# Last gate tile of batch 1 moved to the scan's beginning, reciprocal moved, every second softplus difference made in SBUF

## The chip, the cores and the metric

One NeuronCore of a Trainium2 chip. The time is device microseconds (us) for one execution of the whole kernel. TensorE is PE in the rows (its weight load PEld), VectorE is DVE, ScalarE ACT, GpSimd POOL, SyncE SP. SP and ACT each issue DMAs into a queue of their own.

## The reference

A decoder layer on x of shape (2, 512, 1024): a Mamba block, cross attention over a context of 1024 tokens, and a feed-forward block, each added to its input and followed by a layernorm. The change lies in the Mamba block alone:

```python
proj = hidden_states @ in_proj_w                # -> x and z, each (2, 512, 2048)
xc = silu(causal_conv4(x))                      # depthwise, along the sequence
ssm_p = einsum('bdl,ed->ble', xc, x_proj_w)     # 64 for dt, 16 for B, 16 for C
dt_r, Bm, Cm = rmsnorm of the three pieces
dt = softplus(dt_r @ dt_proj_w.T + dt_bias)     # (2, 2048, 512)
h = exp(dt * A) * h + dt * B * xc               # the scan, 16 states a channel
y = (einsum(h, C) + D * xc) * silu(z)
out = y @ out_proj_w.T
```

Everything is float32. Where a matrix product must be accurate, each operand is split into a rounded part ("hi") and a remainder ("lo"), and three products are summed (`three_passes`, L106).

## The kernel before

The program is written by hand, engine by engine: each engine has one list of instructions, and semaphores order them. A channel tile is 128 channels by 512 tokens; a batch has 16 (`IT`), both have 32 (`NX`).

**The projection stage** (`mamba_in`, 0 to 302 us). PE computes 32 x tiles and then 4 gate (z) tiles of batch 1 (`main(n)`, n = 32 to 35, 24 matmuls each), alternately into PSUM banks 0 and 1. The other gate tiles are made during the scan. Behind each x tile DVE does the convolution in four steps (`conv`, L491, L495), ACT the silu (L392) and the rounding (L398), and PE the x_proj product (`xproj`). Weights come through three slots: SP loads, ACT rounds (`round_w`, L384), POOL makes the remainder (`rest_w`, L599).

After a batch's last x_proj product, ACT squares the result and takes the root (L405 to L410), and DVE normalises (`normalize`: reciprocal L509, products L514 and L515). This frees the dt products on PE (`dt_product(i)`, L684), each for a pair of channel tiles; i = 8 to 15 are batch 1. For each i ACT makes exp(-|v|) (L424, L426) and its logarithm (L434). DVE makes the rounding difference of the exponential (`remainder`: L522 and L524 with the result in PSUM banks 2 and 3 for i >= 8, L527 and L529 with the result in SBUF for i < 8), then `ramp` (L543) and `total` (L549). POOL multiplies the result by xc (`product(i)`, L611), and SP stores dt and u to DRAM.

**The scan** (`mamba_scan`, 302 to 1093 us). 32 iterations (`it`), one a channel tile, of 8 pairs n. For each pair: ACT makes a = exp(dt * A) in PSUM (L1063); POOL makes dbx = u * B (L895); DVE runs the scan (L1092) and multiplies by C (L1081; for two pairs of eight POOL does, L1107); PE sums over the states (L1197). In between PE makes the keys and values of the attention (units "k", L1150, and "v", L1158). The tile it needs dt and u in a spread layout: `load_dt(it)` and `load_u(it)` are four DMAs of 256 KB each.

Iteration 1 needs dt(1) and u(1), which lie over the buffers of x's rounded part and of the dt weights. SP issues these loads (L853) before the key weights wk (1.5 MB, L910), a context chunk (1 MB, L878), the value weights wv (1.5 MB, L912) and a second chunk (1 MB). `product(n)` of the scan on POOL waits for u(it) at the first pair of an iteration, ACT for dt(it).

Of the kernel before, what the change touches and what calls it, by code (L numbers as in the profile page):

```python
# [27 lines left out]
P = 128  # L28
# [84 lines left out]
Projection = namedtuple("Projection", "sync scalar vector gpsimd tensor r_done dt_done")  # L113
# [89 lines left out]
def mamba_in(nc, res, d, ps_all, scan):  # L203
# [51 lines left out]
    par_ld, dtw_ld = sem("par_ld"), sem("dtw_ld")  # L255
# [15 lines left out]
    IN_PSUM = BG  # L271
    BY_POOL = range(IT, NX - 2)
# [11 lines left out]

    def w_tile(n):
        return n % IT if n < NX else IT + n - NX

    def sync(sp):
        def load_w(n):
            if n >= NW:  # L290
                sp.wait_ge(main_done, n - NW + 1)
            sp.dma_start(w[n % NW][:], d["w_in"][w_tile(n)]).then_inc(w_ld[n % NW], 16)

        def load_x(b):
            for k in range(HT):
                sp.dma_start(x[b][:, k], d["x_t"][k, :, b * L:(b + 1) * L]).then_inc(x_ld[b][k], 16)
# [79 lines left out]
        sp.wait_ge(bc_st, 16 * B)  # L376
        sp.wait_ge(z_st, 16 * NF)

    def scalar(act):
        def round_w(n):  # L380
            if n >= NW:
                act.wait_ge(main_done, n - NW + 1)
            act.wait_ge(w_ld[n % NW], 16 * (n // NW + 1))
            nc.scalar.activation(w_hi[n % NW][:], w[n % NW][:], ACT.Copy).then_inc(w_hi_done, 1)  # L384
# [2875 lines left out]
```

## Time and profile before

| | |
|---|---|
| median of 3 runs | 3032.65 us (3032.1 to 3036.48) |
| the profiled execution | 3035.89 us, its span 3034.6 us |
| granted TensorE clock, mean | 0.974 of full speed |
| busy: PE, DVE, ACT, POOL | 93%, 79%, 52%, 60% of the span |
| projection stage | 0 to 302 us |
| scan | 302 to 1093 us |

The profiled execution took 3.2 us more than the median. Rows give start, duration, engine, line, output and input names (buffer numbers left out), and in brackets how long the engine was idle before and who released it. "PEclk" is the granted clock of TensorE: 1.00 is 2.4 GHz, 0.50 is 1.2 GHz. The shares are averages over stages; which engine sets the pace differs from stage to stage.

### The profile page before, as it was taken

How to read it: one execution, taken by the hardware profiler on the slowest of the kernel's cores; microseconds unless marked ns; L12 is line 12 of the kernel's file. 1: busy time of each engine (PE TensorE's matmuls, PEld its weight loads, DVE VectorE, ACT ScalarE, POOL GpSimd, SP SyncE). 2: the span in 40 equal slices, each digit the busy share in tenths (PEclk: the TensorE clock that was granted, in tenths of full speed). 3: DMA queues.
4: the chain of work that ended last, by engine and by line, in shares of the span. 5: the costliest groups of instructions: out<-in, count | busy, mean ns of one | idle time of the engine just before them, and what ended most of it. 6: DMA issues, size and time to landing. Idle time of an engine off the chain costs nothing. (4 is left out here: it accounts for less than half of the span.)

```text
span 3034.6 us, 35492 instructions
## 1 busy us (share of the span) xinstructions
PE 2824.4 (93%) x11950; PEld 2029.5 (67%) x11950; DVE 2386.7 (79%) x2206; ACT 1571.8 (52%) x2722; POOL 1815.3 (60%) x1068
## 2 busy tenths in 40 slices
PE   8996788888788989999999999999989999999997
PEld 6773344343222357888888888878768888887886
DVE  6677999999999968444777777765988888875677
ACT  4566455555665544214888888873433333334443
POOL 3474999999999943403888888861044444430034
PEclk9997899999989999999999999999989999999999
DMA  5457986665875644331111111225245555567654
GB/s 193 125 181 225 290 199 168 175 165 148 263 208 146 197 177 174 118 118 62 35 36 37 37 37 37 71 69 191 92 157 180 181 180 181 180 218 239 195 178 138
DMA packets 221699, 455.41 MB, mean 150 GB/s; under 512 B 34381, under 2 KB 48461, under 8 KB 219661
## 3 DMA queue, kind: packets, MB, share of 16 engines
q1 hardware_dynamic: 184942, 402.27, 42.7%
q10 hardware_dynamic: 36576, 50.87, 5.1%
q8 instruction: 97, 1.59, 0.2%
q14 instruction: 84, 0.69, 0.1%
HBM read 322.89 MB, written 130.15 MB: 149 GB/s over the span
## 5 line engine op out<-in xcount | busy, mean ns | idle before, releaser
L2105 POOL TENSOR_TENSOR at_p_lo<-at_p,at_p_hi 128x512 fp32r<-128x512 f32 x384 | 514.7, 1348 | 241.9 <-ACT at_p_hi L1998 234.1
L895 POOL TENSOR_TENSOR scan_dbx<-scan_u,scan_b_bc 128x1024 f32<-128x1024 f32 x256 | 596.4, 2364 | 1.6 <-DMA scan_u<-u 1.6
L1063 ACT ACTIVATE mamba_ps<-scan_dt,scan_a_neg 128x512 f32<-128x512 f32 (+1 forms) x512 | 332.0, 680 | 313.0 <-DVE scan_g L1081 289.4
L1092 DVE TENSOR_TENSOR_SCAN mamba_ps<-mamba_ps,scan_dbx 128x1024 f32<-128x1024 f32 x195 | 439.9, 2283 | 7.3 <-ACT mamba_ps L1065 6.0
L2025 DVE TENSOR_REDUCE at_neg_max<-heads_ps 128x1 fp32r<-128x1536 f32 x128 | 225.0, 1758 | 134.2 <-PE heads_ps L2117 132.3
L2990 POOL TENSOR_TENSOR ff_raw<-ff_raw,ff_scale 128x512 f32<-128x512 f32 x112 | 116.3, 1069 | 356.2 <-DMA ff_raw<-in_w 247.7
L108 PE MATMUL heads_ps<-ff_x_hi,ff_w_hi 128*128 128x512 f32 x784 | 309.8, 395 | 17.5 <-DVE ff_u L2750 6.6
L109 PE MATMUL heads_ps<-ff_x_lo,ff_w_hi 128*128 128x512 f32 x784 | 307.9, 393 | 0.0
L110 PE MATMUL heads_ps<-ff_x_hi,ff_w_lo 128*128 128x512 f32 x784 | 307.7, 393 | 0.0
L1994 ACT ACTIVATE at_p<-heads_ps 128x512 f32<-128x512 f32 x384 | 228.2, 594 | 109.9 <-PE heads_ps L2141 95.7
L1998 ACT ACTIVATE at_p_hi<-at_p 128x512 fp32r<-128x512 f32 x384 | 242.7, 632 | 12.2
L1167 PE MATMUL mamba_ps<-scan_x,scan_wz 128*128 128x512 f32 x448 | 216.8, 629 | 23.2 <-ACT scan_zb L984 16.1
L1081 DVE TENSOR_TENSOR scan_g<-mamba_ps,scan_c_bc 128x1024 f32<-128x1024 f32 x195 | 234.7, 1204 | 0.0
L1197 PE MATMUL mamba_ps<-scan_g,scan_sel 128*32 128x512 f32 x1024 | 138.5, 611 | 79.1 <-DVE scan_g L1081 65.6
L1167 PEld LDWEIGHTS mamba_ps<-scan_x,scan_wz 128*128 128x128 f32 x448 | 84.1, 198 | 157.4 <-issue 131.3
L108 PEld LDWEIGHTS heads_ps<-ff_x_hi,ff_w_hi 128*128 128x128 f32 x784 | 149.0, 190 | 51.4 <-DVE ff_u L2750 7.4
L109 PEld LDWEIGHTS heads_ps<-ff_x_lo,ff_w_hi 128*128 128x128 f32 x784 | 149.1, 190 | 31.4 <-issue 0.5
L110 PEld LDWEIGHTS heads_ps<-ff_x_hi,ff_w_lo 128*128 128x128 f32 x784 | 149.0, 190 | 31.5
L108 PE MATMUL heads_ps<-ff_hs_hi,ff_w_hi 128*128 128x512 f32 x392 | 154.6, 394 | 7.3 <-DVE ff_act_h L2779 3.7
L2555 ACT ACTIVATE ff_w_hi<-heads_ps 128x512 fp32r<-128x512 f32 x112 | 66.9, 598 | 181.6 <-DVE heads_ps L2739 177.9
L1107 POOL TENSOR_TENSOR scan_g<-scan_g,scan_c_bc 128x1024 f32<-128x1024 f32 x61 | 144.4, 2368 | 27.4 <-DVE scan_g L1092 27.3
L109 PE MATMUL heads_ps<-ff_hs_lo,ff_w_hi 128*128 128x512 f32 x392 | 153.7, 392 | 0.0
(303 smaller groups left out, 6993.2 us busy)
## 6 DMA issues: line engine op xcount, KB each, us to landing
scan_dt<-dt SPq DMA_DIRECT2D x124, 256.0 KB, 4.8
scan_u<-u SPq DMA_DIRECT2D x124, 256.0 KB, 7.6
ff_raw<-in_w SPq DMA_DIRECT2D x56, 512.0 KB, 4.4
ff_down_ar<-ac SPq DMA_DIRECT2D x98, 256.0 KB, 2.7
ff_down_hr<-hc SPq DMA_DIRECT2D x98, 256.0 KB, 2.7
in_w<-in_w_in SPq DMA_DIRECT2D x36, 512.0 KB, 3.8
ff_act_w<-in_w SPq DMA_DIRECT2D x14, 1024.0 KB, 7.3
hc<-ff_act_t SPq DMA_DIRECT2D x56, 256.0 KB, 6.1
```

The costliest lines, as they stand in the source:

```text
L108: nc.tensor.matmul(out, w_hi, x_hi, start=start, stop=False)
L109: nc.tensor.matmul(out, w_hi, x_lo, start=False, stop=False)
L110: return nc.tensor.matmul(out, w_lo, x_hi, start=False, stop=stop)
L895: nc.gpsimd.tensor_tensor(dbx[n % SL][:].rearrange("p (h l) -> p h l", h=2), u[it % 2][:, c:c + 2], b_bc[b][:, k // 2].unsqueeze(1).to_bro ...
L1063: nc.scalar.activation(at[:, h * L + h:(h + 1) * L], dt[it % 2][:, c, h:L], ACT.Exp, scale=a_neg[:, it % IT, e:e + 1]).then_inc(a_ready, 1)
L1081: nc.vector.tensor_tensor(g[n % SG][:].rearrange("p (h l) -> p h l", h=2), ps_a[n % SA].rearrange("p (h l) -> p h l", h=2), c_bc[n // (NP ...
L1092: nc.vector.tensor_tensor_scan(out[:], ps_a[n % SA], dbx[n % SL][:], 0.0, ALU.mult, ALU.add).then_inc(scanned, 1)
L1167: last = nc.tensor.matmul(ps_x, wz[q % ZC][:, k], x[:, k, b * L:(b + 1) * L], start=k == 0, stop=k == HT - 1)
L1994: nc.scalar.activation(p[t % NSL][:], ps_s[t % 2], ACT.Exp, scale=SCALE).then_inc(exp_done, 1)
L1998: nc.scalar.activation(p_hi[t % NSL][:], p[t % NSL][:], ACT.Copy).then_inc(p_hi_done, 1)
L2025: nc.vector.tensor_reduce(neg_max[:, i, HD:HD + 1], ps_mx.rearrange("p n l -> p (n l)"), AX_X, ALU.max, negate=True).then_inc(max_done, 1)
L2105: nc.gpsimd.tensor_tensor(p_lo[n % NSL][:], p[n % NSL][:], f32(p_hi[n % NSL][:]), ALU.subtract).then_inc(p_lo_done, 1)
```

## The change

It does five things.

1. **Beginning.** The convolution's parameters get a semaphore of their own (`conv_ld`). The third weight tile is loaded ahead of the x_proj weights. The split of these weights (ACT L442, DVE L559) moves from before the first convolution to behind the second. The 8 loads of batch 1's x are issued one a tile.
2. **Reciprocal.** `normalize(1)` moves up on DVE, ahead of `remainder(7)` and `ramp(7)`; on ACT `round_w(34)` moves ahead of `squares(1)`.
3. **Softplus of batch 1.** For every odd i >= 8 the difference is made in SBUF, and DVE takes both remainders of a pair of i first, then both ramps and totals. `ps_x`, the banks of the dt products, is in another order, and the waits of `dt_product` follow it.
4. **Last gate tile.** `main(35)` moves from between the dt products to the beginning of PE's scan, behind the last `total`, into bank 3. Its copy (ACT) stands before pair 4 of the scan, its store (SP) behind it.
5. **Loads.** dt(1) and u(1), which lie over what `main(35)` and the dt products read, are issued behind that store, and so behind wk, the first chunk, wv and the second chunk.

The core of the diff:

```diff
-    main_bank = [ps_all[:, n % 2] for n in range(NT)]
+    main_bank = [ps_all[:, n % 2] for n in range(NT - 1)] + [ps_all[:, 3]]
-    ps_x += [ps_all[:, m:m + 2] for m in (6, 4, 6, 4, 0, 6, 4, 0)]
+    ps_x += [ps_all[:, m:m + 2] for m in (6, 4, 0, 6, 4, 0, 6, 4)]
...
+    def in_psum(i):
+        return i >= IN_PSUM and i % 2 == 0
...
         load_w(0)
-        load_x(0)
+        for k in range(HT):
+            load_x(0, k)
         load_w(1)
-        sp.dma_start(cw[:], d["conv_w"]).then_inc(par_ld, 16)
-        sp.dma_start(cb[:], d["conv_b"]).then_inc(par_ld, 16)
+        sp.dma_start(cw[:], d["conv_w"]).then_inc(conv_ld, 16)
+        sp.dma_start(cb[:], d["conv_b"]).then_inc(conv_ld, 16)
+        load_w(2)
...
-        load_w(2)
-        load_x(1)
...
-            if i in (BG + 1, BG + 3):
-                store_gate(2 + (i - BG) // 2)
+            if i == BG + 1:
+                store_gate(2)
             store_u(i)
-        scan.load_dt(sp, 1)
-        scan.load_u(sp, 1)
         for s in range(2):
             sp.wait_ge(u_st[s], 16 * NG // 2)
...
+    def last_store(sp):
+        sp.wait_ge(left, NF)
+        sp.dma_start(d["z"][IT + NF - 1], zf[NF - 1]).then_inc(z_st, 16)
+        sp.wait_ge(main_done, NT)
+        sp.wait_ge(dt_mm, NG)
+        scan.load_dt(sp, 1)
+        scan.load_u(sp, 1)
         sp.wait_ge(z_st, 16 * NF)
+    def last_gate(act):
+        act.wait_ge(u_done, 5)
+        act.wait_ge(xc_st, 16 * (NX - 1))
+        gate(act, NF - 1)
...
-        gate(0)
+        gate(act, 0)
+        round_w(NX + 2)
         squares(1)
         root(1)
-        round_w(NX + 2)
-        gate(1)
-        round_w(NX + 3)
+        gate(act, 1)
         for i in range(BG, NG, 2):
             for n in range(2):
                 exponentials(i + n)
             for n in range(2):
                 logarithm(i + n)
-            if i < BG + 4:
-                gate(2 + (i - BG) // 2)
+                if i == BG and n == 0:
+                    gate(act, 2)
+            if i == BG + 2:
+                round_w(NT - 1)
...
-        for i in range(BG - 2, BG):
-            remainder(i)
-            ramp(i)
+        remainder(BG - 2)
+        ramp(BG - 2)
         normalize(1)
+        remainder(BG - 1)
+        ramp(BG - 1)
         for i in range(BG - 2, BG):
             total(i)
-        for i in range(IN_PSUM, NG):
-            remainder(i)
-            ramp(i)
-            total(i)
+        for i in range(IN_PSUM, NG, 2):
+            for n in range(2):
+                remainder(i + n)
+            for n in range(2):
+                ramp(i + n)
+                total(i + n)
...
-                pe.wait_ge(r_done, (BG + 1, BG + 2, BG + 2, BG + 3, BG + 4, BG + 5)[i - BG - 2])
-                if i == BG + 4:
-                    pe.wait_ge(left, NF)
+                if i == BG + 2:
+                    pe.wait_ge(left, NF - 1)
+                else:
+                    pe.wait_ge(r_done, i - 2)
...
-        main(NX + 2)
-        for i in range(BG + 2, BG + 4):
+        main(pe, NX + 2)
+        for i in range(BG + 2, NG):
             dt_product(i)
-        main(NX + 3)
-        for i in range(BG + 4, NG):
-            dt_product(i)
...
         sp.wait_ge(before.dt_done, IT)
-        load_xs(sp, 1)
         sp.dma_start(wk[:], d["w_k"]).then_inc(wk_ld, 16)
         load_chunk(sp, 0)
         sp.dma_start(wv[:], d["w_v"]).then_inc(wv_ld, 16)
         load_chunk(sp, 1)
+        before.last_store(sp)
+        load_xs(sp, 1)
...
+            if n == 4:
+                before.last_gate(act)
...
         pe.wait_ge(before.dt_done, IT)
+        before.last_main(pe)
```

How SP's queue stands at the scan's beginning, from the store of the last pair of u on; `scan_dt_80` and `scan_u_82` are dt(1) and u(1). Before:

```order
L316 DMA u<-in_uu_151 128x2x512
L853 DMA scan_dt_80<-dt 32x4x512 x4
L853 DMA scan_u_82<-u 32x4x512 x4
L875 DMA scan_xs_99<-xc 128x512
L910 DMA scan_wk<-in_w_k 128x3072
L878 DMA scan_cx_67<-in_ctx 128x8x256
L912 DMA scan_wv<-in_w_v 128x3072
L878 DMA scan_cx_68<-in_ctx 128x8x256
L853 DMA scan_dt_79<-dt 32x4x512 x4
```

And now:

```order
L322 DMA u<-in_uu_151 128x2x512
L939 DMA scan_wk<-in_w_k 128x3072
L908 DMA scan_cx_67<-in_ctx 128x8x256
L941 DMA scan_wv<-in_w_v 128x3072
L908 DMA scan_cx_68<-in_ctx 128x8x256
L387 DMA z<-in_zf_157 128x512
L883 DMA scan_dt_80<-dt 32x4x512 x4
L883 DMA scan_u_82<-u 32x4x512 x4
L905 DMA scan_xs_99<-xc 128x512
```

dt(1), u(1) and the xs tile have moved behind 5 MB of other loads and the gate tile's store.

DVE from the end of batch 1's convolutions: `in_sq` is the reciprocal, `in_ee` the exponential, `in_dd` the SBUF tile of the difference, `mamba_ps` PSUM. Before:

```order
L527 TENSOR_SCALAR in_dd_152<-in_ee_146 128x1024
L529 TENSOR_TENSOR in_dd_152<-in_ee_146,in_dd_152 128x1024
L543 SCALAR_TENSOR_TENSOR in_ll_148<-mamba_ps,in_ll_148 128x1024
L527 TENSOR_SCALAR in_dd_153<-in_ee_147 128x1024
L529 TENSOR_TENSOR in_dd_153<-in_ee_147,in_dd_153 128x1024
L543 SCALAR_TENSOR_TENSOR in_ll_149<-mamba_ps,in_ll_149 128x1024
L509 RECIPROCAL in_sq<-in_rms 96x512
L514 SCALAR_TENSOR_TENSOR in_dtr<-in_ssm,in_lnw,in_sq 64x512
```

And now, down to the first pair of batch 1:

```order
L565 SCALAR_TENSOR_TENSOR in_ll_148<-mamba_ps,in_ll_148 128x1024
L531 RECIPROCAL in_sq<-in_rms 96x512
L536 SCALAR_TENSOR_TENSOR in_dtr<-in_ssm,in_lnw,in_sq 64x512
L537 SCALAR_TENSOR_TENSOR in_ssm<-in_ssm,in_lnw,in_sq 32x512
L549 TENSOR_SCALAR in_dd_153<-in_ee_147 128x1024
L551 TENSOR_TENSOR in_dd_153<-in_ee_147,in_dd_153 128x1024
L565 SCALAR_TENSOR_TENSOR in_ll_149<-mamba_ps,in_ll_149 128x1024
L571 TENSOR_TENSOR in_dd_152<-in_dd_152,in_ll_148 128x1024
L571 TENSOR_TENSOR in_dd_153<-in_dd_153,in_ll_149 128x1024
L544 TENSOR_SCALAR mamba_ps<-in_ee_146 128x1024
L546 TENSOR_TENSOR mamba_ps<-in_ee_146,mamba_ps 128x1024
L549 TENSOR_SCALAR in_dd_152<-in_ee_147 128x1024
```

Three instructions now stand behind the normalisation instead of before it, and the second tile of a pair takes its difference in `in_dd`, not in PSUM.

## Rows read from the trace of the kernel before

**Rows 1.** Windows: busy time (instructions) of PE, PEld, DVE, ACT, POOL; clock; DMA.
```profile
100.00:200.00 100.00, 98.12 (x406) 74.67 (x405) 75.44 (x80) 63.16 (x73) 59.20 (x28) 1.00 0.47 148
400.00:450.00 50.00, 43.17 (x186) 21.07 (x185) 49.72 (x30) 26.57 (x59) 48.15 (x22) 1.00 0.89 222
```

**Rows 2.** Timeline of DVE in the scan: the scans of pairs 8 and 10.
```profile
327.82 2.28 DVE L1092 TENSOR_TENSOR_SCAN scan_g<-mamba_ps,scan_dbx 128x1024 f32<-128x1024 f32 x1
...
336.40 2.30 DVE L1092 TENSOR_TENSOR_SCAN mamba_ps<-mamba_ps,scan_dbx 128x1024 f32<-128x1024 f32 x1 [2.97 <-ACT mamba_ps L1065]
```

**Rows 3.** Timeline of the beginning, PE and DVE.
```profile
18.18 2.62 DVE L559 TENSOR_TENSOR in_xpw_lo<-in_xpw,in_xpw_hi 128x1536 fp32r<-128x1536 f32 x1 [5.92 <-ACT in_xpw_hi L442]
...
24.02 0.47 PE L108 MATMUL mamba_ps<-in_x_hi,in_w_hi 128*128 128x512 f32 x1 [2.58 <-DVE in_acc L495]
...
31.22 0.39 PE L108 MATMUL mamba_ps<-in_xc_hi,in_xpw_hi 128*96 128x512 f32 x1
```

**Rows 4.** Timeline around batch 1's normalisation: ACT, DVE, POOL, PE.
```profile
236.66 0.69 ACT L410 ACTIVATE in_rms<-mamba_ps,in_eps 96x512 f32<-96x512 f32 x1
...
239.14 3.34 DVE L509 RECIPROCAL in_sq<-in_rms 96x512 f32<-96x512 f32 x1
...
242.22 2.34 POOL L599 TENSOR_TENSOR in_w_lo<-in_w,in_w_hi 128x1024 fp32r<-128x1024 f32 x1 [1.46 <-ACT in_w_hi L384]
...
242.51 2.59 DVE L514 SCALAR_TENSOR_TENSOR in_dtr<-in_ssm,in_lnw,in_sq 64x512 f32<-64x512 f32 x1
...
245.31 7.17 PE L684 MATMUL mamba_ps<-in_dtr,in_dtw 65*128 65x512 f32 x8 [4.74 <-issue]
```

**Rows 5.** Timeline of DVE: a difference in SBUF, and two tiles in PSUM.
```profile
233.16 0.68 DVE L527 TENSOR_SCALAR in_dd<-in_ee 128x1024 f32<-128x1024 f32 x1
233.87 1.23 DVE L529 TENSOR_TENSOR in_dd<-in_ee,in_dd 128x1024 f32<-128x1024 f32 x1
...
292.20 1.23 DVE L522 TENSOR_SCALAR mamba_ps<-in_ee 128x1024 f32<-128x1024 f32 x1
...
297.18 1.23 DVE L522 TENSOR_SCALAR mamba_ps<-in_ee 128x1024 f32<-128x1024 f32 x1
```

**Rows 6.** Timeline of POOL and DVE in batch 0, where both work in SBUF.
```profile
157.27 2.37 POOL L611 TENSOR_TENSOR in_uu<-in_dd,xc 128x1024 f32<-128x1024 f32 x1
...
158.03 2.69 DVE L549 TENSOR_TENSOR in_dd<-in_dd,in_ll 128x1024 f32<-128x1024 f32 x1
```

**Rows 7.** Timeline of POOL: the last two products of u.
```profile
297.15 2.34 POOL L611 TENSOR_TENSOR in_uu<-in_dd,xc 128x1024 f32<-128x1024 f32 x1 [2.63 <-DVE in_dd L549]
...
306.38 2.35 POOL L611 TENSOR_TENSOR in_uu<-in_dd,xc 128x1024 f32<-128x1024 f32 x1
```

**Rows 8.** Timeline of SP: the last store of u and the loads behind.
```profile
308.76 0.36 SPq L316 DMA_DIRECT2D u<-in_uu x1
309.16 2.23 SPq L853 DMA_DIRECT2D scan_dt<-dt x4
...
314.01 0.42 SPq L910 DMA_DIRECT2D scan_wk<-in_w_k x1
```

**Rows 9.** Landing of u(1), issued 311.4 to 312.9, by tile.
```profile
L853 SPq DMA_DIRECT2D scan_u<-u x4: 432/432/432, 311.4 to 312.9; - x4
...
DMA to landing us min/median/max: 6.4/7.5/8.5
```

**Rows 10.** Landing of u(2), issued 330.6 to 333.0, by tile.
```profile
L853 SPq DMA_DIRECT2D scan_u<-u x4: 430/433/1424, 330.6 to 333.0; - x4
...
DMA to landing us min/median/max: 11.2/12.3/13.6
```

**Rows 11.** Landing of the last store of u, issued at 308.76, by tile.
```profile
DMA to landing us min/median/max: 3.0/3.0/3.0
```

**Rows 12.** Timeline of PE: first key unit and first value unit.
```profile
328.25 5.81 PE L1150 MATMUL mamba_ps<-scan_cx,scan_wk 128*128 128x256 f32 x16 [1.39 <-DMA scan_cx<-in_ctx]
...
334.99 5.43 PE L1158 MATMUL mamba_ps<-scan_wv,scan_cx 128*128 128x384 f32 x16
```

More of the change, by code:

```diff
@@ L290, in load_w, with load_x @@
             if n >= NW:
[L291 to L296, printed above, removed]
+                sp.wait_ge(main_done, n - NW + 1 if n < NT - 1 else NX + 2)
+            sp.dma_start(w[slot(n)][:], d["w_in"][w_tile(n)]).then_inc(w_ld[slot(n)], 16)
+        def load_x(b, k):
+            sp.dma_start(x[b][:, k], d["x_t"][k, :, b * L:(b + 1) * L]).then_inc(x_ld[b][k], 16)
         def store_conv(n):
@@ L376, in sync, with gate @@
         sp.wait_ge(bc_st, 16 * B)
-        sp.wait_ge(z_st, 16 * NF)
+        sp.wait_ge(z_st, 16 * (NF - 1))
+    def last_store(sp):
[5 more added lines that the diff above has]
+        scan.load_u(sp, 1)
+        sp.wait_ge(z_st, 16 * NF)
+    def gate(act, m):
+        act.wait_ge(main_done, NX + m + 1)
+        nc.scalar.activation(zf[m], main_bank[NX + m], ACT.Copy).then_inc(left, 1)
+    def last_gate(act):
+        act.wait_ge(u_done, 5)
+        act.wait_ge(xc_st, 16 * (NX - 1))
+        gate(act, NF - 1)
     def scalar(act):
@@ L440, in scalar @@
         round_w(2)
-        act.wait_ge(par_ld, 16 * 7)
-        nc.scalar.activation(xpw_hi[:], xpw[:], ACT.Copy).then_inc(xpw_hi_done, 1)
         for n in range(NX):
@@ L458, in scalar @@
             round_xc(n)
+            if n == 0:
+                act.wait_ge(par_ld, 16 * 5)
+                nc.scalar.activation(xpw_hi[:], xpw[:], ACT.Copy).then_inc(xpw_hi_done, 1)
             group, step = divmod(n + 1 - FIRST_GROUP, 4)
@@ L614, in gpsimd @@
             rest_w(n)
-        for n in range(1, NX + 2):
+        for n in range(1, NX + 1):
             rest_w(n + 2)
@@ L629, in gpsimd, with main, last_main @@
             product(i)
-    def tensor(pe):
-        def main(n, between=None, at=0):
-            b = n // IT if n < NX else B - 1
-            if n == 0:
-                pe.wait_ge(w_lo_first, 1)
-            else:
-                pe.wait_ge(w_lo_done, n)
-            if NX <= n - 2:
-                pe.wait_ge(left, n - NX - 1)
-            elif n >= 2:
-                pe.wait_ge(conv_step, KC * (n - 1))
-            for k in range(HT):
-                if n % IT == 0 and n < NX:
-                    pe.wait_ge(x_lo_done[b], k + 1)
-                if between is not None and k == at:
-                    between()
-                last = three_passes(nc, main_bank[n], w_hi[n % NW][:, k], w_lo[n % NW][:, k], x_hi[b][:, k], x_lo[b][:, k],
-                                    k == 0, k == HT - 1)
-            last.then_inc(main_done, 1)
+    def main(pe, n, between=None, at=0):
+        b = n // IT if n < NX else B - 1
+        if n == 0:
+            pe.wait_ge(w_lo_first, 1)
+        else:
+            pe.wait_ge(w_lo_done, n)
+        if n >= NX + 2:
+            pe.wait_ge(left, n - NX - 1)
+        elif n >= 2:
+            pe.wait_ge(conv_step, KC * (n - 1))
+        for k in range(HT):
+            if n % IT == 0 and n < NX:
+                pe.wait_ge(x_lo_done[b], k + 1)
+            if between is not None and k == at:
+                between()
+            last = three_passes(nc, main_bank[n], w_hi[slot(n)][:, k], w_lo[slot(n)][:, k], x_hi[b][:, k], x_lo[b][:, k],
+                                k == 0, k == HT - 1)
+        last.then_inc(main_done, 1)
+    def last_main(pe):
+        main(pe, NT - 1)
+    def tensor(pe):
         def xproj(n):
@@ L695, in tensor @@
             if n == IT + 1:
-                main(n, lambda: mean_squares(0), 2)
+                main(pe, n, lambda: mean_squares(0), 2)
             elif n == FIRST_GROUP:
-                main(n, lambda: products(0), 4)
+                main(pe, n, lambda: products(0), 4)
             else:
-                main(n)
+                main(pe, n)
             if n >= IT and n < IT + 2:
```

68 lines of the change are left out of this document (37 added, 31 removed).

## The prediction

> **What bounds the kernel now.** I read the windows table first, then the timelines of the stretches that the diff touches, last SP's queue and the landing times. In the projection stage PE sets the pace: 98.12 of 100 us busy between 100 and 200 [rows 1]. From 245 to 302 us it is no longer PE but the softplus chain of batch 1 (PE dt product, ACT exponential and logarithm, DVE four passes, POOL product). In the scan it is DVE, 49.72 of 50 us busy, with POOL at 48.15 right beside it [rows 1]. DVE's last sizeable idle time there is 2.97 us before pair 10 [rows 2]; from 336.40 on it works without a break for hundreds of us. So everything earlier has to be measured at one point: the start of pair 10's scan, 336.40 us. What the change takes from that instant comes off the end; what comes later is fixed DVE work.
>
> **The beginning.** Before, DVE did the split of the x_proj weights at 18.18 to 20.8 us and only then the first convolution, and PE's third tile waited for it 2.58 us and started at 24.02 [rows 3]. It then got half clock for a while, and the first x_proj product came at 31.22. A full-clock tile is 24 matmuls at 0.228 us a step, 5.5 us; so 24.02 + 5.5 = 29.5, and 1.7 us went to the clock. Now the first convolution follows the first tile (15.2 us), and the third tile follows the second at 21.3. It ends at 26.8. The x_proj product then waits for the split, which stands behind the second convolution: 21.5 + 3.1 + 0.7 for the remainder of xc + 1.7 = 27.0. Gain 31.22 - 27.05 = 4.2 us; if the clock falls all the same, 2.5. PE has no idle time to swallow it until the end of batch 1.
>
> **The normalisation.** The root is done at 237.35, but DVE starts the reciprocal at 239.14, since two more passes stand before it; now it starts at 237.45, 1.7 us sooner. The next pass, L514, took 2.59 us because POOL was in the middle of a weight remainder [rows 4]; its smaller twin L515 takes 0.74. That remainder (of the last gate tile) is gone from there, and the one before it is earlier, so I take 0.75: 1.8 us less. Together the dt weights' operand is ready at 241.6, not 245.1: 3.5 us. PE's wait of 4.74 us [rows 4] shrinks to 1.2, so the first dt products keep the full clock (8 passes in 3.6 us instead of 7.17).
>
> **The softplus.** From the operand (245.1) to the end of the seventh total, when POOL starts `product(14)` (297.15 [rows 7]), 52.05 us pass. A tile with its difference in PSUM costs DVE 4.98 us (292.20 to 297.18), a pair 9.96. In SBUF the first pass costs 0.71, not 1.27 [rows 5], and the pairing hides one dependency: 9.2 for a pair. But now DVE and POOL meet. In batch 0 `total` took 2.69 us instead of 1.22: it began at 158.03 and ended 1.1 us after POOL's product (157.27 to 159.64) [rows 6]. Both inputs of the new odd `total` lie in SBUF, and POOL begins `product(i)` at the very moment when `total(i)` ends; ramp(i+1) hides 1.15 of its 2.35 us, the rest, 1.2 us, DVE waits. A pair costs 10.4 us. By rows: first pair's differences done at 254.05 (its SBUF pass waits for POOL's products 6 and 7), then 1.26 + 1.14 for ramp and total 8, then three pairs of 10.4: 287.65. From the operand at 241.6 that is 46.05 us, 6.0 less than before: one gate tile no longer stands between the dt products, the other runs at full clock and is done before ACT wants it, and DVE no longer waits for either; what the faster pass saves is more than given back to POOL.
>
> The Trainium skill (SBUF — State Buffer, section "SBUF: two separate sides") says that a VectorE instruction with two SBUF inputs and a GpSimd one exclude each other for the whole instruction. The trace agrees, 2.69 us against 1.22. Without that rule the pair would be 9.2 us and the result 3.6 us lower.
>
> Sum at POOL's `product(14)`: 4.2 + 3.5 + 6.0 = 13.7 us sooner, 283.45 instead of 297.15.
>
> **The loads of dt(1) and u(1).** Here the gain is given back. Before: `product(15)` on POOL ended at 308.73, the store was issued at 308.76, and dt(1) and u(1) directly behind it; u(1) was complete at 312.9 + 8.5 = 321.4 [rows 8, 9], before POOL wanted it (324.8). Now SP waits first for that store to land (3.0 us [rows 11]), then issues wk, chunk, wv, chunk (5 MB), the gate store, and only then dt(1) and u(1). What such a train costs, the trace shows: from the landing of u(1), 321.4, to that of u(2), 333.0 + 13.6 = 346.6 [rows 10], 25.2 us, the queue carried the same: one small tile, the 5 MB, dt and u. With the start from an idle queue, 0 to 2 us, I take 26.2. The chain from `product(14)` at P: 2.35, a wait for DVE's last total 1.1, three dbx 6.98, `product(15)` 2.35, store landing 3.1: the train starts at P + 15.9, u(1) is there at P + 42.1. Then POOL's dbx of pair 8 (2.4) and on DVE the scan of 8, the product of 7 and the scan of 9 (2.2 + 1.1 + 2.2): pair 10 at P + 50.0. Before it was 336.40 - 297.15 = 39.25. Lost 10.75 us. In this is counted that the 2.97 us before pair 10 go: they came from a key unit late for its chunk (1.39 us [rows 12]), which now lands first.
>
> By the Trainium skill (DMA: Bandwidth & Descriptors, "Queues, rings and completion order") each DMA engine takes the descriptors of a ring in order. By that rule nothing lets u(1) pass, and the sum stands; if the loads shared the engines instead, rival 1 would be near. The landing of u(2) behind the second chunk agrees with the rule.
>
> **PE after that wait.** The value unit stands before the sum of pairs 8 and 9, which the scan of pair 12 needs, and can start only after the product of 7, that is after the stall, on a PE that idled some 8 us. Before it took 5.43 us at full clock and the key unit 5.81 us, of which 3.7 would be full clock [rows 12]. So 2.1 us more, little of it hidden: 2.0. Bounds: 0 if the clock stays up, 5.4 if all of it is at half.
>
> **Hidden.** The last gate tile on PE, 5.5 to 10.3 us, lies in the time in which PE waits for the first sum (302.15 + 1.9 to 313.38 before); its copy on ACT (0.6) before pair 4 has 4 us of cover, and both are in front of the stall. The extra weight rounding on ACT (1.05) is covered as ACT needs 8.9 of the 10.4 us of a pair. Without this cover it would be 1.
>
> **Sum.** 13.7 - 10.75 - 2.0 = 0.95 us sooner at pair 10 to 12. On the profile's execution 3035.89 - 0.95 = 3034.9; on the median, 3.2 us lower, 3031.7. I forecast 3031.7.
>
> **Rivals.**
> 1. *The loads do not wait.* If u(1) lands by POOL's time (wk and the chunks share, or the train is shorter than by the rows), 13.7 - 1.1 for the lock + 2.97 for the gap = 15.6 us, 3017; halfway, 3024. For it: dt(1)'s pieces landed within 4.0 to 5.7 us in an empty queue. Against: u(2)'s pieces took 11.2 to 13.6, standing behind the chunk.
> 2. *Slower: PE at half clock.* With the last gate tile gone from between the dt products, PE has only 1.8 us of work for each wait. If its clock falls there, a dt product costs 3.6 us (rows 4: 7.17 for two), ACT's exponentials come 1.7 us later each, a pair is 12 us and not 10.4 (+5 over three pairs), the later start moves the train too, and the value unit costs 5.4 instead of 2.0: 3031.7 + 5 + 3.4 = 3040. It decides from a pair of 11.5 us on. Against: DVE has 1 to 2 us slack over ACT by the sums above.
> 3. *The beginning gives nothing* (the third tile waits for weights instead): 3035.9, no change.
>
> **Chances.** Forecast 0.62, its own range 3026 to 3037; rival 1 0.20; rival 2 0.11; rival 3 0.07. A measurement of this kernel tells a change from 0.2%, 6.1 us, on. Faster by more: 0.20 and the lower edge of the forecast 0.05, 0.25. Slower: 0.11 and 0.01, 0.12. Within: 0.63. The range for 8 in 10, 3020 to 3038.5, leaves out the full rival 1 and half of rival 2.
>
> **What would show it.** Right: the first x_proj product at about 27 us; the reciprocal directly behind the root and L514's like at 0.75 us; odd totals of some 2.4 us; POOL's last product but one at about 283; POOL idle 8 to 11 us before the dbx of pair 8, released by the DMA of u; no gap before pair 10; pair 10's scan at about 333.5. Wrong: POOL not idle there, then rival 1; pairs of 12 us with a granted clock of 0.50 at the dt products, then rival 2; a later gap of DVE in the scan that I have not seen.

## The result: 0.26% slower, and the profile after

| | before | after |
|---|---|---|
| median, 7 runs each | 3032.1 us (3030.55 to 3036.48) | 3039.78 us (3037.06 to 3045.0) |
| ratio | | 1.0026, 95% interval 1.0016 to 1.0036 |
| profiled execution | 3035.89 us | 3038.82 us |

The forecast was 3031.7 us. The changed kernel is 7.7 us slower by the medians; the forecast is 8.1 us too low, outside its range.

I read the profile after at the points that the prediction named. In all rows below, tile i stands for the pair of channel tiles i (`total(i)`, `product(i)`). First the beginning and the normalisation (timeline of PE and DVE; columns as in the rows of before):

```profile
26.99 0.45 PE L108 MATMUL mamba_ps<-in_xc_hi,in_xpw_hi 128*96 128x512 f32 x1 [0.20 <-DVE in_xpw_lo L587]
...
233.22 3.35 DVE L531 RECIPROCAL in_sq<-in_rms 96x512 f32<-96x512 f32 x1 [1.15 <-ACT in_rms L434]
236.61 0.74 DVE L536 SCALAR_TENSOR_TENSOR in_dtr<-in_ssm,in_lnw,in_sq 64x512 f32<-64x512 f32 x1
```

The first x_proj product stands at 26.99 (forecast 27.05; [rows 3] 31.22). The reciprocal follows the root at once and L536 takes 0.74 us, so the operand of the dt products is there at 237.35; the forecast's 241.6 less the 4.2 of the beginning is 237.4.

Then the softplus of batch 1 (timeline of DVE and POOL):

```profile
252.43 0.69 DVE L549 TENSOR_SCALAR in_dd<-in_ee 128x1024 f32<-128x1024 f32 x1 [6.33 <-DMA dt<-in_dd]
...
268.29 2.34 DVE L571 TENSOR_TENSOR in_dd<-in_dd,in_ll 128x1024 f32<-128x1024 f32 x1
...
273.02 2.35 POOL L626 TENSOR_TENSOR in_w_lo<-in_w,in_w_hi 128x1024 fp32r<-128x1024 f32 x1
273.14 2.78 DVE L549 TENSOR_SCALAR in_dd<-in_ee 128x1024 f32<-128x1024 f32 x1
...
290.44 2.34 POOL L638 TENSOR_TENSOR in_uu<-in_dd,xc 128x1024 f32<-128x1024 f32 x1 [4.93 <-DVE in_dd L571]
```

`product(14)` starts at 290.44 where 283.45 was forecast. Two waits were not in the forecast. The difference of tile 9 waits 6.33 us for a DMA: it is written over dt(6), and the store of dt(6) has not landed. And the difference of tile 13 takes 2.78 us instead of 0.69, beside POOL's remainder of the last gate tile. The odd total takes 2.34 us, as forecast.

Why dt(6) is not stored yet shows SP's timeline and the landing time of the store issued at 242.40:

```profile
237.38 2.02 SPq L890 DMA_DIRECT2D scan_b_bc<-bc  x4
...
239.45 2.80 SPq L890 DMA_DIRECT2D scan_c_bc<-bc  x4
...
242.40 1.52 SPq L318 DMA_DIRECT2D dt<-in_dd  x2
```
```profile
who waited for it (us, times):
  DVE in_dd L549: 6.3, 1
...
DMA to landing us min/median/max: 10.0/10.0/10.0
```

Eight spread loads of B's and C's rows stand ahead of it. The last store of u, on an idle queue, landed in 3.0 us [rows 11]; this one in 10.0.

Last the scan's beginning: POOL, then SP with the landing time of u(1), then DVE and PE:

```profile
332.46 9.26 POOL L925 TENSOR_TENSOR scan_dbx<-scan_u,scan_b_bc 128x1024 f32<-128x1024 f32 x4 [13.24 <-DMA scan_u<-u]
```
```profile
303.12 0.36 SPq L322 DMA_DIRECT2D u<-in_uu  x1
305.88 0.34 SPq L939 DMA_DIRECT2D scan_wk<-in_w_k  x1
...
317.81 2.06 SPq L883 DMA_DIRECT2D scan_u<-u  x4
```
```profile
DMA to landing us min/median/max: 10.7/11.6/13.0
```
```profile
334.84 2.29 DVE L1125 TENSOR_TENSOR_SCAN scan_g<-mamba_ps,scan_dbx 128x1024 f32<-128x1024 f32 x1 [12.57 <-POOL scan_dbx L925]
...
338.16 4.47 DVE L1125 TENSOR_TENSOR_SCAN mamba_ps<-mamba_ps,scan_dbx 128x1024 f32<-128x1024 f32 x2
...
348.99 2.29 DVE L1125 TENSOR_TENSOR_SCAN scan_g<-mamba_ps,scan_dbx 128x1024 f32<-128x1024 f32 x1 [1.93 <-PE mamba_ps L1231]
```
```profile
340.25 6.65 PE L1191 MATMUL mamba_ps<-scan_wv,scan_cx 128*128 128x384 f32 x16
```

With P for the start of `product(14)`, 290.44: the train of loads (the key weights first, at 305.88) starts at P + 15.4 (forecast 15.9), POOL gets u(1) at P + 42.0 (42.1), pair 10 (the second of the two scans from 338.16) starts at P + 49.9 (50.0), and before pair 12 DVE waits 1.93 us for the sum behind the value unit (2.0). This half came as forecast.

The differences between executions of one kernel matter here. A second profile of the kernel before (its run stands below) shows what the first one hid. Windows table, 22 to 30 us, of the first profile and of the second (columns as in [rows 1]):

```profile
22.00:30.00 8.00, 5.97 (x19) 4.82 (x20) 7.82 (x9) 5.40 (x8) 3.03 (x2) 0.79 0.59 181
```
```profile
22.00:30.00 8.00, 6.24 (x28) 5.11 (x29) 7.38 (x9) 5.12 (x8) 2.50 (x2) 1.00 0.59 187
```

The first had a granted clock of 0.79 there and its first x_proj product at 31.22; the second 1.00, and 29.29. All later points up to pair 12 are 2 us sooner in the second: P at 295.25, pair 12 at 341.02. Pair 12 of the changed kernel, 348.99, is 8.0 us behind the second profile and 6.0 behind the first. Not all of that reaches the end: DVE's first instruction behind the scan starts at 1106.66 in the changed kernel, 5.9 us behind the second profile (1100.80) and 3.4 behind the first (1103.22), since DVE's waits between pair 12 and there differ from profile to profile. The medians differ by 7.7 us.

### The profile page after: what moved, and what is told of

The parts are those of the page before. It is cut to its first block and busy times, and to the rows that moved or that the text cites. A ratio compares the mean times of both kernels' runs of the same rounds, so it can differ in the third digit from the quotient of the medians.

```text
span 3037.5 us, 35491 instructions
## 1 busy us (share of the span) xinstructions
PE 2820.3 (93%) x11950; PEld 2024.7 (67%) x11950; DVE 2383.9 (78%) x2206; ACT 1570.7 (52%) x2722; POOL 1814.9 (60%) x1068
## 5 line engine op out<-in xcount | busy, mean ns | idle before, releaser
L1125 DVE TENSOR_TENSOR_SCAN scan_g<-mamba_ps,scan_dbx 128x1024 f32<-128x1024 f32 x61 | 138.9, 2277 | 21.5 <-POOL scan_dbx L925 16.0
```

Source lines behind the costliest of these rows:

```text
L1125: nc.vector.tensor_tensor_scan(out[:], ps_a[n % SA], dbx[n % SL][:], 0.0, ALU.mult, ALU.add).then_inc(scanned, 1)
```

## The experiments

Four points tell most of each run: the time from the end of batch 1's root to P, from P to pair 12's scan, where pair 12 stands, and where the scan ends (DVE's first instruction behind it). All were read from one profile of each; the last columns are the timed runs, with the ratio to the kernel before on the same chip.

| kernel | root to P | P to pair 12 | pair 12 | scan's end | median | ratio (95% interval) |
|---|---|---|---|---|---|---|
| before, the profile shown | 59.8 | 45.9 | 343.0 | 1103.2 | 3032.1 | 1 |
| before, second profile | 59.8 | 45.8 | 341.0 | 1100.8 | | |
| changed | 57.2 | 58.6 | 349.0 | 1106.7 | 3039.8 | 1.0026 (1.0016 to 1.0036) |
| first_loads | 56.7 | 49.7 | 339.9 | 1097.0 | 3032.0 | 0.9993 (0.9982 to 1.0005) |
| store_ahead | 57.5 | 58.3 | 349.5 | 1107.2 | 3044.4 | 1.0034 (1.0023 to 1.0045) |
| all_psum | 48.7 | 57.4 | 340.1 | 1105.1 | 3032.9 | 0.9998 (0.9987 to 1.0008) |
| late_loads | 59.7 | 57.2 | 352.3 | 1117.2 | 3049.5 | 1.0050 (1.0036 to 1.0064) |
| rows_later | 55.3 | 58.9 | 347.3 | 1112.4 | 3041.4 | 1.0024 (1.0014 to 1.0034) |
| tile_by_tile | 52.4 | 59.8 | 345.2 | 1106.0 | 3039.0 | 1.0016 (1.0006 to 1.0025) |
| begin_alone | 59.8 | 45.9 | 339.2 | 1098.9 | 3028.8 | 0.9987 (0.9977 to 0.9996) |
| recip_alone | 54.7 | 46.8 | 339.1 | 1103.2 | 3030.4 | 0.9991 (0.9983 to 1.0) |
| order_alone | 59.8 | 43.7 | 341.1 | 1106.0 | 3031.1 | 0.9996 (0.9987 to 1.0005) |
| loads_spread_out | 47.8 | 43.6 | 325.8 | 1085.0 | 3015.5 | 0.9940 (0.9927 to 0.9953) |
| the same, second run | 48.6 | 44.5 | 326.6 | 1086.7 | 3017.2 | 0.9945 (0.9931 to 0.9959) |

From pair 12 to the scan's end the profiles take between 757.2 and 765.1 us, so a gain or a loss of a few us at pair 12 can be hidden there: the runs below tell where that happened, and the last section returns to it.

My theory: the three losses above (store of dt(6), POOL beside SBUF passes, train of loads) make the whole difference up to pair 12.

**first_loads: the train of loads.**

```diff
+    def early_loads(sp):
+        sp.wait_ge(main_done, NT)
+        sp.wait_ge(dt_mm, NG)
+        scan.load_dt(sp, 1)
+        scan.load_u(sp, 1)
...
+        before.early_loads(sp)
+        load_xs(sp, 1)
         sp.dma_start(wk[:], d["w_k"]).then_inc(wk_ld, 16)
```

> The changed kernel with dt(1), u(1) and the xs tile loaded ahead of the key weights, as soon as the last gate tile and the dt products are done on PE. Theory A (the stall before pair 8 is the load train): product(14) stays where it is in the changed kernel (290.4), u(1) lands some 24 us behind it instead of 42, POOL does not wait more than 1 us for it, DVE's idle time of 12.6 us before pair 8 goes, but the first key unit again waits for its chunk (a gap of about 3 us before pair 10); pair 10 at 290.4 + 39.3 + 1.1 for the lock = 330.8 instead of 340.35, and the value unit at full clock gives 2 more: the whole 9 to 11.5 us less than the changed kernel, about 3029. Rival (the order of loads does not matter, the wait would only move to the key unit or to the chunk): pair 10 within 3 us of 340, the whole within 3 us of 3039.8.

Measured: P at 290.20, POOL has no wait for u(1), but the gap before pair 10 is 5.66 us, not 3, since the key unit waits 3.79 us for its chunk (timeline of PE and DVE):

```profile
324.80 6.10 PE L1186 MATMUL mamba_ps<-scan_cx,scan_wk 128*128 128x256 f32 x16 [3.79 <-DMA scan_cx<-in_ctx]
...
333.23 2.30 DVE L1128 TENSOR_TENSOR_SCAN mamba_ps<-mamba_ps,scan_dbx 128x1024 f32<-128x1024 f32 x1 [5.66 <-ACT mamba_ps L1101]
```

Pair 12 is 9.1 us sooner than in the changed kernel, the median 7.8 us lower, where 9 to 11.5 were expected. The order of loads matters, and the rival falls; but in this order the key unit's chunk is late, as u(1) was in the other.

**late_loads: the same from the other side.** Kernel before, `load_dt(1)`, `load_u(1)` and `load_xs(1)` moved behind the second `load_chunk`.

> The kernel before with only dt(1), u(1) and the xs tile loaded behind both chunks. Theory A (a train of 26 us stands ahead of u(1), and its price is what the prediction said): u(1) lands some 42 us behind product(14) (297.15), POOL and DVE wait for it before pair 8, pair 10 at 297.15 + 49.9 - 1.1 = 346 instead of 336.4, and the value unit 1.9 more: the whole 10 to 12 us more, about 3043.5. Rival (part of the stall of the changed kernel comes from its other edits, its gate store before the loads and its last gate tile): 3 to 7 us more, below 3039.

Measured: POOL gets u(1) at P + 40.3 (335.41 - 295.11) and waits 12.6 us for it; P to pair 12 is 57.2 against 45.8, 11.4 us more. So the order of loads by itself makes most of the 12.7 us that the changed kernel loses there; the other 1.3 were not tested apart. The median is 16.7 us higher, above the 10 to 12 expected, and so is the scan's end, by 16.4 against the second profile. Its profile holds later waits of DVE that the second profile of before does not have:

```profile
404.13 2.29 DVE L1092 TENSOR_TENSOR_SCAN scan_g<-mamba_ps,scan_dbx 128x1024 f32<-128x1024 f32 x1 [2.56 <-ACT mamba_ps L1065]
430.15 2.29 DVE L1092 TENSOR_TENSOR_SCAN scan_g<-mamba_ps,scan_dbx 128x1024 f32<-128x1024 f32 x1 [1.68 <-ACT mamba_ps L1065]
553.26 2.29 DVE L1092 TENSOR_TENSOR_SCAN scan_g<-mamba_ps,scan_dbx 128x1024 f32<-128x1024 f32 x1 [1.54 <-PE mamba_ps L1197]
627.36 2.29 DVE L1092 TENSOR_TENSOR_SCAN scan_g<-mamba_ps,scan_dbx 128x1024 f32<-128x1024 f32 x1 [1.24 <-ACT mamba_ps L1065]
```

Together 7.0 us; the second profile of before has only smaller ones of its own, 1.96 and 0.81 us (shown under before_again). I return to them at the end.

**store_ahead: one store past the rows.** Changed kernel, `store_dt(6)` and `store_dt(7)` ahead of `scan.load_rows(sp, 0)`.

> The changed kernel with SP's stores of dt(6) and dt(7) issued ahead of the eight loads of B's and C's rows, and nothing else. Theory A (the softplus step failed first because the difference of tile 9 is written over dt(6), whose store stood behind those loads for 10 us): the first SBUF pass of tile 9 no longer waits 6.3 us for the DMA, the store lands within 4 us, product(14) comes about 4.5 us sooner (286 instead of 290.4), all that follows moves with it, the whole 4 to 5 us less, about 3035. Rival (the wait is covered, since ACT's exponential of tile 11 or POOL's products are late there anyway): another wait of about 6 us takes its place and the whole is within 1.5 us of 3039.8.

Measured: the expectation fails, and the rival has the mechanism right: another wait takes the place of the first. Tile 9 waits for no DMA, but tile 11 waits 4.26 us for the store of dt(8), which landed 9.1 us after its issue:

```profile
246.53 2.63 DVE L549 TENSOR_SCALAR in_dd<-in_ee 128x1024 f32<-128x1024 f32 x1
...
259.47 4.64 POOL L638 TENSOR_TENSOR in_uu<-in_dd,xc 128x1024 f32<-128x1024 f32 x2 [10.85 <-DMA u<-in_uu]
...
262.06 2.60 DVE L549 TENSOR_SCALAR in_dd<-in_ee 128x1024 f32<-128x1024 f32 x1 [4.26 <-DMA dt<-in_dd]
```

POOL, too, waits 10.85 us for a store of u. Root to P stays at 57.5. So it is not this one store: the queue is full in that stretch. The DMA view of the changed kernel, 236 to 262 us; the second line is SP's queue, whose packets took 86.5% of the time of the 16 DMA engines:

```profile
DMA packets 2759, 6.88 MB, mean 265 GB/s; under 512 B 304, under 2 KB 304, under 8 KB 2502
...
q1 hardware_dynamic: 2758, 6.86, 86.5%
```

The median is 3044.4 us, 4.6 above the changed kernel's, though pair 12 stands only 0.5 us later. The profiled execution was the fastest of the nine (3039.4), so the profile does not show what the others lose; the two intervals overlap.

**rows_later: the rows out of that stretch.** Changed kernel, `scan.load_rows(sp, 0)` behind tile 9's `store_u`.

> The changed kernel with the eight loads of B's and C's rows (2 MB written) moved behind the stores of tile 9, and nothing else. Theory B (between 237 and 262 us SP's queue carries more than it can move, so moving one store ahead only made the next one late; the rows are the part that can wait): the difference of tile 9 does not wait for a DMA, nor does that of tile 11 by more than 1 us, POOL's product(8) does not wait 10 us for a store of u; product(14) at 286 or sooner, pair 12 4 to 5 us sooner than 348.99, the whole 4 to 6 us less than the changed kernel. Rival (the queue is full in any case, the rows' place does not matter): product(14) at 289 to 291, the whole within 1.5 us of 3039.8.

Measured: half. The store of tile 8 now lands in 2.7 us and neither tile 9 nor tile 11 waits for a store, but the rows, now issued at 258.5, hold up later ones: tile 13 waits 2.95 us for the store of dt(10), and tile 15 1.51 us for that of dt(12).

```profile
271.98 0.69 DVE L550 TENSOR_SCALAR in_dd<-in_ee 128x1024 f32<-128x1024 f32 x1 [2.95 <-DMA dt<-in_dd]
```

Root to P 55.3, 2.0 us less; 4.5 were expected. The median did not fall: pair 12 is 1.7 us sooner, but the scan's end 5.7 us later, behind four waits like those of late_loads (2.66, 1.73, 1.54 and 1.26 us).

**all_psum: the SBUF difference undone.**

```diff
     def in_psum(i):
-        return i >= IN_PSUM and i % 2 == 0
+        return i >= IN_PSUM
...
             for n in range(2):
                 remainder(i + n)
-            for n in range(2):
                 ramp(i + n)
                 total(i + n)
```

> The changed kernel with the difference of every tile of batch 1 made in PSUM again, and remainder, ramp and total tile by tile; the other four parts stay. Theory A (the SBUF difference costs three things: the wait for a place whose store is late, 4.5 us, POOL's weight remainder holding DVE, 2.1, and the lock of every odd total, some 0.4 a pair): product(14) at about 282 instead of 290.4, pair 10 also 1.1 sooner for the lock beside the early products that goes; the whole 8 to 9 us less, about 3031. Rival (the SBUF difference is worth its shorter pass and the loss of 7 us in the softplus comes from the dt products at half clock): the pair in PSUM is 10.4 us or more, product(14) at 288 or later, the whole no more than 2.5 us less.

Measured: P at 282.70, root to P 48.7, pair 12 at 340.14, 8.9 us sooner than in the changed kernel. Timeline of DVE, one tile and the start of the next:

```profile
266.14 1.23 DVE L544 TENSOR_SCALAR mamba_ps<-in_ee 128x1024 f32<-128x1024 f32 x1
267.40 1.23 DVE L546 TENSOR_TENSOR mamba_ps<-in_ee,mamba_ps 128x1024 f32<-128x1024 f32 x1
268.54 1.22 DVE L565 SCALAR_TENSOR_TENSOR in_dd<-mamba_ps,in_ll 128x1024 f32<-128x1024 f32 x1
269.79 1.22 DVE L571 TENSOR_TENSOR in_dd<-in_dd,mamba_ps 128x1024 f32<-128x1024 f32 x1
271.12 1.23 DVE L544 TENSOR_SCALAR mamba_ps<-in_ee 128x1024 f32<-128x1024 f32 x1
```

4.98 us a tile with no wait. This is the largest single finding: the SBUF difference with its pairing costs 8.6 us of root to P. The median, 3032.9, is 6.9 us below that of the changed kernel; by the ratios, each to the kernel before on its own chip, it is some 8.5. Expected were 8 to 9. What is left of the change makes root to P 11.1 us shorter than before; recip_alone below gives 5.1 of them, and the other 6.0, by subtraction, belong to the gate tile's move and the new order of the banks, which no run takes alone.

**tile_by_tile: SBUF without the pairing.** Changed kernel, remainder, ramp and total of a tile before the next tile, odd differences still in SBUF.

> The changed kernel with the differences of odd tiles still in SBUF, but remainder, ramp and total tile by tile instead of two remainders first. It separates the SBUF place from the pairing. Theory C (the pairing asks for the reused place some 5 us sooner, and that is what the store cannot meet; it also leaves POOL's weight remainder beside an SBUF difference): tile 9 waits at most 1 us for the DMA instead of 6.3, the weight remainder lies beside PSUM passes; but each odd difference now waits for POOL's product of the even tile, so a pair costs 11.0 us instead of 10.35: product(14) at 290.4 - 4.9 - 2.1 - 0.4 + 2.0 = 285, pair 12 5 to 6 us sooner than 348.99, the whole 4 to 6 us less than the changed kernel, 3034.5. Rival (SBUF itself costs it, by the lock beside POOL's products in either order): product(14) at 289 or later and the whole within 2 us of 3039.8.

Measured: P at 285.44 (285 expected). Tile 9 waits 2.70 us, not 6.33 (at most 1 was expected), and the weight remainder (271.52) lies beside PSUM passes.

```profile
252.33 0.69 DVE L549 TENSOR_SCALAR in_dd<-in_ee 128x1024 f32<-128x1024 f32 x1 [2.70 <-DMA dt<-in_dd]
```

So of the 8.6 us, 4.8 come with the pairing and 3.8 remain with SBUF alone. But behind P 1.2 us are lost again, pair 12 is only 3.8 us sooner, and the median is 0.8 us lower (3 by the ratios), where 4 to 6 were expected; the later waits appear here as well (1.54 and 1.23 us).

**begin_alone and recip_alone: the first two parts by themselves.** The kernel before with the edits of part 1, and with those of part 2.

> The kernel before with the first part of the change alone (parameters' own semaphore, third weight tile sooner, the split behind the second convolution, batch 1's x loads one a tile). Theory A: the first x_proj product at 27.05 instead of 31.22, the 4.2 us go unchanged through the projection stage, where PE has no idle time (product(14) at 293.0), and through the scan (pair 12 at 338.8): the whole 4.2 us less, 3028.5, if no clock dip differs. Rival (it is lost where batch 1's normalisation waits for the stores, or in the loads): product(14) at 296 or later, the whole within 1.5 us of before.

> The kernel before with the second part alone (reciprocal of batch 1 ahead of tile 7's difference and ramp, the rounding of the gate weights ahead of the squares). Theory A: the dt products' operand 3.5 us sooner (241.6 instead of 245.1) and the first dt products at full clock for part; product(14) 3 to 3.5 us sooner, 294, and the whole 3 to 3.5 us less, 3029.5. Rival (the softplus chain of the first pairs waits for ACT, whose exponential table and gate copies do not move, so half or more is lost): product(14) less than 2 us sooner, the whole within 2 us of before.

Measured: the first part gives 3.9 us at pair 12 against the profile shown and 1.8 against the second profile; its median is 3.4 us below that of before. The second part gives 5.1 us from root to P (3 to 3.5 expected), of which 1.0 is lost behind P, and 1.8 us of median; its profile has waits of 2.49 and 3.33 us behind pair 12. The first gain is small but clear of no change (0.9977 to 0.9996); the interval of the second reaches 1.0.

**order_alone: a third order of loads on the kernel before.**

```diff
+            if i == NG - 1:
+                scan.load_wk(sp)
             store_u(i)
+        scan.load_chunk(sp, 0)
         scan.load_dt(sp, 1)
         scan.load_u(sp, 1)
+        scan.load_xs(sp, 1)
```

> The kernel before with the new order of loads alone (key weights ahead of the last store of u, first chunk directly behind it, then dt(1), u(1), xs). Theory: the only thing it can give is DVE's 2.97 us before pair 10, which came from the first key unit waiting 1.4 us for its chunk at a low clock; u(1) lands at about product(14) + 27, still in time; pair 10 at product(14) + 36.3 instead of 39.25, the whole 3 us less, 3029. So the rest of the 17 us of the best version comes from batch 1's part and not from here. Rival (u(1) is late behind the chunk): POOL waits 1 us or more before pair 8 and the whole is within 1.5 us of before or slower.

Measured: the gap before pair 10 is gone, but POOL waits 1.42 us for u(1), so both theories are half right: P to pair 12 is 2.1 us shorter. The median falls by 1.4 us, but the interval of the ratio includes 1.

**loads_spread_out: the better version.** The changed kernel with all_psum's edit and this order (SP waits for `main_done` and `dt_mm`, the end of the gate tiles and of the dt products on PE, ahead of dt(1)).

> All differences of batch 1 in PSUM (as in the run where that stood alone), and the loads in a third order: the key weights go out before the last store of u (they need only the last total), the first chunk directly behind that store, then dt(1), u(1) and the xs tile without waiting for the store to land, then the value weights and the second chunk. Theory (each load stood in the way of another one; the queue has 9 us of nearly idle time between the last two stores of u): product(14) at 282.7, u(1) there at product(14) + 27, about when POOL wants it (27.7), the first key unit no longer waits for its chunk, so no gap before pair 10; pair 10 at 282.7 + 36.3 = 319, pair 12 at 325.6 against 343.0 before: 17 us less than before, 3015.5. Rival (the bandwidth of that stretch is the bound and not the order): POOL or PE waits 3 us or more for u(1) or the chunk, the whole 3020 to 3026. A second rival: what is gained here comes back as short stretches of PE at half clock later on; then pair 12 is at 326 and the whole still above 3022.

Measured: P at 282.15 (282.7), pair 10 at 319.13 (319), pair 12 at 325.78 (325.6), median 3015.48 (3015.5). Timeline of DVE and PE, where pair 10 had waited:

```profile
311.93 4.87 PE L1186 MATMUL mamba_ps<-scan_cx,scan_wk 128*128 128x256 f32 x16
...
319.13 2.30 DVE L1128 TENSOR_TENSOR_SCAN mamba_ps<-mamba_ps,scan_dbx 128x1024 f32<-128x1024 f32 x1 [0.57 <-ACT mamba_ps L1101]
```

It beats both kernels: 0.9940 (0.9927 to 0.9953). One of its five executions took 8945 us, with a clock of 1.0; so I ran it again.

> The same kernel as the run with loads spread out, a second time, since one of its five executions took 8945 us. If that came from the kernel, a part of its executions is again above 3100 us; if it was a disturbance from outside, all are at 3013 to 3020 us. Pair 12 again at 325.8 and the ratio to before 0.9935 to 0.995.

Measured: 3017.22 us median, 3013.02 to 3019.9, 5 runs, ratio 0.9945 (0.9931 to 0.9959), pair 12 at 326.64. The long execution did not come again in these five; what it was stays open.

**before_again: how much one profile can be trusted.**

> The kernel before, one more profile. Its first profile was 3.2 us above the median. If what differs between executions of one kernel is single stretches of PE at the lower clock in the scan, the waits of DVE between 345 and 1090 us, or the clock in the later stages, differ by as much as the time, while pair 12 stands within 2.5 us of 343.0 and product(14)'s distance to it is the same 45.9 us.

Measured: 3032.63 us, and pair 12 as told under the result. P to pair 12 is 45.8 again. DVE's waits between 345 and 1090 us do not differ as the time does: they sum to 9.0 us here and 9.4 in the profile shown, while the times differ by 3.3. What differs is their place. The profile shown has

```profile
539.38 2.29 DVE L1092 TENSOR_TENSOR_SCAN scan_g<-mamba_ps,scan_dbx 128x1024 f32<-128x1024 f32 x1 [1.54 <-PE mamba_ps L1197]
613.45 2.29 DVE L1092 TENSOR_TENSOR_SCAN scan_g<-mamba_ps,scan_dbx 128x1024 f32<-128x1024 f32 x1 [1.21 <-ACT mamba_ps L1065]
```

and the second one

```profile
634.91 2.29 DVE L1092 TENSOR_TENSOR_SCAN scan_g<-mamba_ps,scan_dbx 128x1024 f32<-128x1024 f32 x1 [1.96 <-ACT mamba_ps L1065]
...
793.97 2.29 DVE L1092 TENSOR_TENSOR_SCAN scan_g<-mamba_ps,scan_dbx 128x1024 f32<-128x1024 f32 x1 [0.81 <-PE mamba_ps L1197]
```

Of the 3.3 us between the two executions, 2.0 lie before pair 12, 0.4 between it and the scan's end, and 0.9 behind the scan.

## Why the prediction was wrong

*Beginning: right, on a base that not every execution has.* 4.2 us against the profile shown, as forecast. But 1.9 of them stand against a dip of the granted clock, which three of five profiles with the old beginning have; against the second profile the gain is 2.3. The prediction saw the dip ("1.7 us went to the clock") and still carried the whole 4.2 to the median. All nine profiles with the new beginning have a clock of 1.00 from 22 to 30 us, so a part of the dip may be a true gain: begin_alone's median is 3.4 us lower.

*Normalisation: right.* The operand came at 237.35 as forecast, and recip_alone shows the gain reaching P, with 5.1 us even more than the 3.5. The first dt products kept the full clock (eight passes in 3.67 us at 237.56, 3.6 forecast).

*Softplus: the step that failed.* The prediction has the "first pair's differences done at 254.05 (its SBUF pass waits for POOL's products 6 and 7)" and "three pairs of 10.4", 6.0 us less from the operand to P; normalisation and softplus together make 9.5 from the root to P. Measured 2.5, so 7.0 us are missing, and pair 12 stands 6.9 us behind the forecast (348.99 against 343.04 - 0.95). What failed is that the prediction let the SBUF pass of tile 9 wait for POOL's products alone, put the wait for the store of dt(6) at nothing, and put nothing beside the pass of tile 13. By the trace: the wait for the store of dt(6), 6.33 us, of which some 1.8 would have gone to POOL's products anyway, costs 4.5; POOL's weight remainder 2.1; the store of dt(12) 0.3. The pairs are 10.35 us where nothing disturbs them, as forecast. all_psum shows the counterpart: with the differences in PSUM root to P is 11.1 us shorter than before, more than the 9.5 that the prediction gave to both parts. What I overlooked is that the SBUF difference is written into the place that the PSUM version needs only at `ramp`, and the pairing brings it forward once more; I asked which engine stands beside the pass and not what must have left its destination. That the lock with POOL (a pass of DVE taking longer while POOL works in SBUF) would cost something I had priced for the odd totals, but not for the last gate tile's remainder, which now stands among POOL's products (L653) and has no price in the prediction.

The lock itself is as told: 2.34 us for an odd total, and 2.78 and 2.63 for a pass of 0.69 beside POOL. The Trainium skill (SBUF — State Buffer, "SBUF: two separate sides") names two kinds of VectorE operation for the exclusion: one with two SBUF inputs, and one in a 2-port perf mode. The prediction used only the first. L549 reads one tile and writes one, and took 2.78 us at 273.14; the trace agrees with the second kind as far as it goes, since the same pass takes 0.69 us into SBUF and 1.23 into PSUM (L544), which fits a faster mode when both its tiles are in SBUF.

*Loads of dt(1) and u(1): right.* 10.75 us forecast; pair 10 at P + 49.9 against P + 39.25 is 10.7. late_loads, on the other kernel, gives P + 40.3 at POOL, first_loads takes the stall away. The sign given with it, POOL idle for 8 to 11 us, was off: it idled 13.24 us, near the 14.4 that the forecast's own numbers give (42.1 less the 27.65 from P to 324.8).

*PE after the wait: the size right, the reason in part.* 2.0 forecast, 1.93 measured. But the value unit took 6.65 us against 5.43, 1.2 longer and not 2.1; the rest is its later start, 0.15 us before pair 10 instead of 1.41. That the two make just 2 us is luck. The granted clock was 0.50 from 330 to 340 us and 0.73 from 340 to 345.

*Behind pair 12, and from the profile to the median: wrong, partly in the other direction.* The premise that "what comes later is fixed DVE work" did not hold: between 345 and 1090 us DVE waits 9.4 us in the profile that the prediction read, 9.0 in the second one, and 6.6 in the changed kernel from 352 on. From pair 12 to the scan's end the changed kernel's profile takes 757.7 us where the profile shown takes 760.2. So the whole profiled execution is only 3.9 us above the 3034.9 forecast, not 6.9. The other 4.2 of the 8.1 us lie between profile and median: the prediction took off 3.2, and the changed kernel's profile lies 1.0 below its own median. That the softplus's 7.0 us look like nearly the whole miss of 8.1 is therefore partly luck; what they explain is the 6.9 at pair 12.

*Rivals.* Rival 1 (no wait for the loads) did not happen; in first_loads, where POOL has no wait, it is worth 9.1 us at pair 12. Rival 2 has the right sign and nearly the right time, 3040, for the wrong reason: the dt products did run at the lower clock (7.17 us for eight passes at 266.02, as in [rows 4]), but undisturbed pairs took 10.35 us and not 12. Rival 3 did not happen.

## What to carry to other kernels

Moving a pass from one memory to another changes what its destination must wait for: ask who reads that place last, when that read (here a store behind 2 MB of other loads) is over, and whether the pass now stands earlier than the one that used to ask. Then look at SP's queue as a whole: where it was full, moving one transfer ahead only moved the wait, and a stretch in which it was idle (here before the last store of u) took a large load without a new wait. And take two profiles of the kernel before where 2 us matter, and compare them to the end: a gain read against a dip of the clock is there only in the executions that have the dip, and a point early in the kernel does not tell the waits behind it.

## What the runs showed of the hardware

In the profiles, executions of one kernel differ by single waits and not by a general slowness. The old beginning has two levels: the first x_proj product at 29.3 us (two profiles, clock 1.00 from 22 to 30 us) or at 31.2 to 31.6 us (three profiles, clock 0.79). In the scan, DVE's waits before the same pairs came with nearly the same sizes in four kernels, each profiled once (2.60 and 1.70, then 1.54 and 1.25 us in all_psum; 2.56, 1.68, 1.54, 1.24 in late_loads; order_alone and rows_later likewise) and are absent in others. Windows table of all_psum around the first of them, and PE's key unit inside it:

```profile
370.00:380.00 10.00, 8.37 (x24) 3.06 (x24) 10.00 (x7) 4.44 (x10) 9.50 (x5) 1.00 0.80 177
380.00:390.00 10.00, 8.03 (x28) 5.38 (x32) 9.37 (x6) 4.08 (x9) 10.00 (x5) 0.66 0.67 184
```
```profile
383.04 6.63 PE L1182 MATMUL mamba_ps<-scan_cx,scan_wk 128*128 128x256 f32 x16 [1.27 <-ACT scan_zb L1014]
```

The granted clock is 0.66 there, the unit takes 6.63 us instead of 3.72, and DVE waits for the exponential behind it. PE had idled 1.93 us and then 1.27 us just before. But that idle time does not decide it: the kernel before has the same 1.93 and 1.26 us at this place, and there the unit is fast:

```profile
385.41 3.72 PE L1150 MATMUL mamba_ps<-scan_cx,scan_wk 128*128 128x256 f32 x16 [1.26 <-ACT scan_zb L984]
```

Why one profile has these stretches and another not, the runs do not show, nor how much of the spread of the kernel before, 3026.6 to 3040.7 us over all its timed runs, comes from them.
